# Cross-attention with a routed feed-forward: value products in blocks of two steps, a rewritten unit order, and two steps moved to ScalarE

## The reference

```python
def _L0_xattn_ref(target, source, target_mask, source_mask, Wq, bq, Wk, bk, Wv, bv):
    q = jnp.einsum('oc,bct->bot', Wq, target) + bq[None, :, None]
    k = jnp.einsum('oc,bcs->bos', Wk, source) + bk[None, :, None]
    v = jnp.einsum('oc,bcs->bos', Wv, source) + bv[None, :, None]
    # 16 heads of 16 channels
    dot = jnp.einsum('bhdt,bhds->bhts', q, k) / math.sqrt(HEAD_DIM)
    mask = target_mask[:, :, :, None] * source_mask[:, :, None, :]
    dot = mask * dot - (1.0 - mask) * NEG
    amap = jax.nn.softmax(dot, axis=-1) * mask
    out = jnp.einsum('bhts,bhds->bhdt', amap, v)
    return out.reshape(b, HEADS * HEAD_DIM, t)

def _L0_ffn_ref(hidden_states, gate_w, w1, w2):
    logits = jnp.einsum('th,eh->te', x, gate_w)
    topw, sel = jax.lax.top_k(jax.nn.softmax(logits, axis=-1), 2)
    topw = topw / jnp.sum(topw, axis=-1, keepdims=True)
    g, u = jnp.split(jnp.einsum('th,eoh->eto', x, w1), 2, axis=-1)
    expert_out = jnp.einsum('eti,ehi->eth', jax.nn.silu(g) * u, w2)
    # weighted by topw and summed over the two experts of each row

x = x + _L0_xattn_ref(_layernorm(x), ctx_2048, mask, mask, Wq, bq, Wk, bk, Wv, bv)
x = x + _L0_ffn_ref(_layernorm(x), gate_w, w1, w2)
```

## Time and profile before

| | |
|---|---|
| median of 3 runs | 867.57 us (867.37 to 872.44) |
| the profiled execution | 871.53 us, span 869.7 us |
| TensorE busy | 801.8 us, 92% |
| VectorE busy | 553.6 us, 64% |
| ScalarE busy | 318.6 us, 37% |
| GpSimd busy | 370.3 us, 43% |
| mean granted TensorE clock | 0.972 of full speed |

### The profile page before, as it was taken

The page is one execution under the profiler, slowest core; times in us unless marked ns, Lnnn a source line. Parts: engine busy times, 40 slices in busy tenths (PEclk is TensorE's granted clock), DMA queues, the critical chain, the costliest instruction groups (busy, mean ns, idle before and its releaser), DMA issues. The chain is left out here.

```text
span 869.7 us, 13002 instructions
## 1 busy us (share of the span) xinstructions
PE 801.8 (92%) x3757; PEld 365.1 (42%) x3758; DVE 553.6 (64%) x1071; ACT 318.6 (37%) x619; POOL 370.3 (43%) x392
## 2 busy tenths in 40 slices
PE   5888898989999998999989988899999999999993
PEld 2322332333333433433333332365555665665661
DVE  5778887889888887888877874445433333333331
ACT  0035465556565565665655666522000000000000
POOL 7544364556565655655745423334211221211221
PEclk9579999999999999999999999999999999999997
DMA  6745577666766866856845542354648546354332
GB/s 188 231 129 145 172 203 221 200 209 210 231 206 184 264 196 182 257 163 177 244 127 160 172 113 83 94 144 110 152 89 227 133 110 172 65 156 72 72 51 34
DMA packets 84524, 138.02 MB, mean 159 GB/s; under 512 B 14765, under 2 KB 40685, under 8 KB 84474
## 3 DMA queue, kind: packets, MB, share of 16 engines
q1 hardware_dynamic: 68970, 108.65, 41.8%
q0 software_dynamic: 7744, 17.86, 10.7%
q10 hardware_dynamic: 7760, 10.89, 4.5%
HBM read 77.36 MB, written 59.36 MB: 157 GB/s over the span
## 5 line engine op out<-in xcount | busy, mean ns | idle before, releaser
L843 ACT ACTIVATE pr<-sc 128x512 f32<-128x512 f32 x512 | 267.1, 603 | 219.5 <-PE sc L1507 219.3
L990 DVE TENSOR_REDUCE mx<-tile 128x2 f32<-128x1024 f32 x256 | 309.0, 1216 | 55.9 <-PE tile L1519 50.3
L1507 PE MATMUL sc<-qk 100*128 100x512 bf16 x512 | 154.8, 384 | 9.9 <-DMA qk<-mxt 7.2
L1519 PE MATMUL tile<-qk 97*128 97x512 bf16 x496 | 150.9, 388 | 14.0 <-DVE mx L990 7.9
L765 POOL DMA_INDIRECT out_dram<-xin,ids x36 | 56.4, 1566 | 224.0 <-DVE ids L1312 220.0
L1545 PE MATMUL pvb<-pr,vp 128*32 128x512 f32 x1024 | 138.0, 611 | 0.0
L1660 PE MATMUL pvb<-wring,qkf 128*128 (+1 forms) x216 | 98.7, 593 | 1.6 <-DVE qkf L1322 1.6
L720 POOL TENSOR_SCALAR parts<-qkf 128x512 bf16<-128x512 f32 x31 | 46.9, 1512 | 123.3 <-DVE qkf L1074 119.3
L1519 PEld LDWEIGHTS tile<-qk 97*128 97x128 bf16 x496 | 35.0, 98 | 145.6 <-issue 75.7
L1639 PE MATMUL tile<-wring,xh 128*128 x288 | 91.3, 460 | 0.0
L1639 PE MATMUL sc<-wring,xh 128*128 x288 | 91.2, 459 | 0.0
(11 more groups left out here) (158 smaller groups left out, 789.1 us busy)
## 6 DMA issues: line engine op xcount, KB each, us to landing
qk<-stack_d SPq DMA_DIRECT2D x32, 768.0 KB
stack_d<-parts SPq DMA_DIRECT2D x32, 384.0 KB, 3.1
wring<-w_dram SPq DMA_DIRECT2D x32, 352.0 KB, 7.2
cin<-routed_d ACTq DMA_DIRECT2D x36, 257.0 KB, 3.6
stack_d<-parts SPq DMA_DIRECT2D x32, 256.0 KB, 3.1
pv_d<-ov SPq DMA_DIRECT2D x32, 256.0 KB, 3.4
xin<-x_dram SPq DMA_DIRECT2D x16, 256.0 KB, 5.4
cin<-ctxt_dram SPq DMA_DIRECT2D x8, 512.0 KB, 6.3
```

Source lines behind the costliest of these rows:

```text
L843: nc.scalar.activation(pr[s % 2][:, j, :], sc[(32 * u + 4 * s + j) % NSC][:, :], ACT.Exp, scale=SCALE).then_inc(exped.sem, 1)
L990: dve.tensor_reduce(cols, t[:, :, :], X, ALU.max, negate=True).then_inc(drained.sem, 1)
L1507: nc.tensor.matmul(sc[(32 * u + 4 * s + j) % NSC][:, :], ks[half(u)][0:ALL_ROWS, h, c * P:c * P + P], qs[half(u)][0:ALL_ROWS, h, :], start ...
L1519: last = nc.tensor.matmul(t[:, i, :], qs[half(w)][0:RAW_ROWS, h, c * P:c * P + P], ks[half(w)][0:RAW_ROWS, h, :], start=True, stop=True)
```

## The change

The first two units (`FRONT`) keep their loop, now in `front_events` and `front`. For units 2 to 15, `STEADY` gives the list of tiles, and TensorE's and VectorE's steps are written out. These are the differences:

- products come in blocks of two steps: 6 and 7 of the unit before behind the first scores, 0 and 1 in step 2, 2 and 3 in step 4, 4 and 5 in step 6. `pr` has three buffers for it (`NPR`); the mask rows `mall` and `mrow` now lie in `ov`;
- values move from step 0 to step 1, `xT` into step 4, logits into step 5. The choice stands ahead of the transpose of the maxima, the keys right behind it and ahead of step 7, and two raw pairs at the unit's end. The raw pairs are spread anew;
- ScalarE normalizes the inputs (`normalize`, for which GpSimd's `batch_rstd` makes a third small value, `shift`), behind the exponentials of step 1. VectorE writes the token rows once, and ScalarE copies them for the second expert (`token_twin`), behind the exponentials of step 3. `choose` reads the logits from PSUM without the copy `lg`;
- on VectorE the reciprocals come ahead of the token normalization, and in unit 15 `plan_early` stands ahead of both. On GpSimd `token_rstd` stands ahead of `values_out`. Product 6 of unit 15 too stands behind the first gate.

```diff
+NPR = 3
+STEADY = (0, 1, 2, "v", 3, 4, 5, 6, "q", "xT", 7, 8, 9, 10, "logits", 11, 12, "maxT", "k", 13, "ranks", 14, 15)
...
+def pair_of(n, i):
+    m = LEAD + i
+    return (n + 1, m) if m < NPAIR else (n + 2, m - NPAIR)
...
+def tile_events(n):
+    if 0 <= n < len(FRONT):
+        return front_events(n)
+    ahead = {"v": 1, "q": 3, "k": 3, "xT": -2, "logits": -2, "ranks": -2, "maxT": 1}
+    ev = []
+    for name in STEADY:
+        if name == "xT" and n == TAIL:
             ev.append((n, "early"))
+        if name == "maxT":
+            if has(n + 1):
+                ev.append((n, ("maxT", n + 1, ALL)))
+        elif name in ahead:
+            if has(n + ahead[name]):
+                ev.append((n, name))
+        elif has(pair_of(n, name)[0]):
+            ev.append((n, ("max", *pair_of(n, name))))
+    if n == LAST - 1:
+        ev.append((n, "count"))
...
-        rstd = Count(sem("rstd"), of(5, "eps", "pow"))
+        rstd = Count(sem("rstd"), lambda n: ["eps", "pow"] + ["shift"] * (n > 0) if has(n + 5) else [])
...
+                if u > 0:
+                    pool.wait_ge(rstd.sem, rstd.at(u, "pow"))
+                    pool.tensor_scalar(at[:, 10:11], at[:, 6:7], at[:, 8:9], -1.0, ALU.mult, ALU.mult
+                                       ).then_inc(rstd.sem, 1)
+                    pool.wait_ge(rstd.sem, rstd.at(u, "shift"))
...
                     part(u, 1)
+                if has(u - 2):
+                    token_rstd(u)
                 if has(u + 1):
                     values_out(u)
-                if has(u - 2):
-                    token_rstd(u)
                 if has(u - 3):
...
+            def token_twin(u):
+                act.wait_ge(normed2.sem, normed2.at(u, "n"))
+                nc.scalar.activation(xa[:, half(u), 1, 0:T], xa[:, half(u), 0, 0:T], ACT.Copy
+                                     ).then_inc(twin.sem, 1)
+            def normalize(u):
+                w = u + 5
+                if not has(w):
+                    return
+                at = ln[:, half(w), :]
+                act.wait_ge(rstd.sem, rstd.at(u, "shift"))
+                if (due := ready.at(w - 7 + half(w + 1), "q")) is not None:
+                    act.wait_ge(ready.sem, due)
+                nc.scalar.activation(xh[:, parity(w), half(w), :], xin[:, half(w), :], ACT.Identity,
+                                     bias=at[:, 10:11], scale=at[:, 8:9]).then_inc(normed.sem, 1)
...
-                            if j == 0 and (due := pved.at(u, s, back=2)) is not None:
+                            if j == 0 and (due := pved.at(u, s, back=NPR)) is not None:
                                 act.wait_ge(pved.sem, due)
-                            nc.scalar.activation(pr[s % 2][:, j, :], sc[(32 * u + 4 * s + j) % NSC][:, :],
+                            nc.scalar.activation(pr[(8 * u + s) % NPR][:, j, :], sc[(32 * u + 4 * s + j) % NSC][:, :],
...
+                    if s == 1 and u > 1:
+                        normalize(u - 1)
+                    if s == 3 and has(u - 2):
+                        token_twin(u)
...
-                if step == 0:
-                    dve.tensor_copy(lg[:, :], tile_of(u, "logits")[:, 0, 0:E]).then_inc(drained.sem, 1)
                 if step == 1:
-                    dve.wait_ge(drained.sem, drained.at(u, "logits"))
                     if (due := gate_exp.at(u - 1, "e")) is not None:
                         dve.wait_ge(gate_exp.sem, due)
-                    dve.max(v8[:, :], lg[:, :]).then_inc(choice.sem, 1)
+                    dve.max(v8[:, :], tile_of(u, "logits")[:, 0, 0:E]).then_inc(choice.sem, 1)
                 if step == 2:
                     dve.wait_ge(choice.sem, choice.at(u, "v8"))
-                    dve.max_index(i8[:, :], v8[:, :], lg[:, :]).then_inc(choice.sem, 1)
+                    dve.max_index(i8[:, :], v8[:, :], tile_of(u, "logits")[:, 0, 0:E]).then_inc(drained.sem, 1)
                 if step == 3:
-                    dve.wait_ge(choice.sem, choice.at(u, "i8"))
+                    dve.wait_ge(drained.sem, drained.at(u, "logits"))
                     dve.tensor_copy(i8f[:, :], i8[:, :]).then_inc(choice.sem, 1)
...
-                maximum(u, u + 1, 4)
-                normalize(u - 1)
-                maximum(u, u + 1, 5)
+                maximum(u, *pair_of(u, 0))
+                maximum(u, *pair_of(u, 1))
+                maximum(u, *pair_of(u, 2))
                 values_out(u)
-                maximum(u, u + 1, 6)
+                maximum(u, *pair_of(u, 3))
                 token_stats(u, 0)
-                maximum(u, u + 1, 7)
                 token_stats(u, 1)
-                maximum(u, u + 1, 8)
-                token_normalize(u, 0)
-                maximum(u, u + 1, 9)
-                token_normalize(u, 1)
                 if u == TAIL:
                     plan_early()
-                maximum(u, u + 1, 10)
+                maximum(u, *pair_of(u, 4))
+                maximum(u, *pair_of(u, 5))
                 reciprocals(u, 0)
-                maximum(u, u + 1, 11)
+                maximum(u, *pair_of(u, 6))
                 reciprocals(u, 1)
+                token_normalize(u)
                 projection_out(u, 0)
-                maximum(u, u + 1, 12)
-                maximum(u, u + 1, 13)
+                batch_stats(u, 0)
+                batch_stats(u, 1)
+                maximum(u, *pair_of(u, 7))
+                maximum(u, *pair_of(u, 8))
+                maximum(u, *pair_of(u, 9))
+                maximum(u, *pair_of(u, 10))
                 choose(u, 0)
                 choose(u, 1)
                 choose(u, 2)
                 choose(u, 3)
-                maximum(u, u + 1, 14)
-                batch_stats(u, 0)
-                maximum(u, u + 1, 15)
-                batch_stats(u, 1)
+                maximum(u, *pair_of(u, 11))
+                maximum(u, *pair_of(u, 12))
                 choose(u, 4)
                 choose(u, 5)
+                split_maxima(u, u + 1, ALL)
+                projection_out(u, 1)
+                maximum(u, *pair_of(u, 13))
+                rows_of(u, 0)
+                rows_of(u, 1)
                 if u == TAIL:
                     fetch(0, 0)
-                maximum(u, u + 2, 0)
-                maximum(u, u + 2, 1)
-                split_maxima(u, u + 1, ALL)
-                maximum(u, u + 2, 2)
-                rows_of(u, 0)
-                maximum(u, u + 2, 3)
-                rows_of(u, 1)
-                projection_out(u, 1)
+                maximum(u, *pair_of(u, 14))
+                maximum(u, *pair_of(u, 15))
...
+            def unit(u):
+                scores(u, 0, 0)
+                scores(u, 0, 1)
+                scores(u, 0, 2)
+                raw(u, 0)
+                scores(u, 0, 3)
+                if u > len(FRONT):
+                    product(u - 1, 6)
+                product(u - 1, 7)
+                raw(u, 1)
+                scores(u, 1, 0)
+                raw(u, 2)
+                scores(u, 1, 1)
+                scores(u, 1, 2)
+                scores(u, 1, 3)
+                values(u)
+                raw(u, 3)
+                scores(u, 2, 0)
+                scores(u, 2, 1)
+                scores(u, 2, 2)
+                raw(u, 4)
+                product(u, 0)
+                product(u, 1)
+                if u == TAIL:
+                    count_early()
+                scores(u, 2, 3)
+                raw(u, 5)
+                scores(u, 3, 0)
+                scores(u, 3, 1)
+                raw(u, 6)
+                scores(u, 3, 2)
+                scores(u, 3, 3)
+                project(u, 0)
+                scores(u, 4, 0)
+                scores(u, 4, 1)
+                transpose_tokens(u)
+                scores(u, 4, 2)
+                raw(u, 7)
+                scores(u, 4, 3)
+                raw(u, 8)
+                product(u, 2)
+                product(u, 3)
+                raw(u, 9)
+                scores(u, 5, 0)
+                scores(u, 5, 1)
+                scores(u, 5, 2)
+                raw(u, 10)
+                scores(u, 5, 3)
+                logits(u)
+                scores(u, 6, 0)
+                scores(u, 6, 1)
+                raw(u, 11)
+                scores(u, 6, 2)
+                raw(u, 12)
+                scores(u, 6, 3)
+                product(u, 4)
+                product(u, 5)
+                if has(u + 1):
+                    transpose_maxima(u, u + 1, ALL)
+                project(u, 1)
+                if u == TAIL:
+                    transpose_rows(0, 0)
+                scores(u, 7, 0)
+                raw(u, 13)
+                scores(u, 7, 1)
+                ranks(u)
+                scores(u, 7, 2)
+                scores(u, 7, 3)
+                raw(u, 14)
+                raw(u, 15)
...
+            product(TAIL, 6)
             product(TAIL, 7)
```

110 lines of the change are left out of this document (47 added, 63 removed).

## The result

The changed kernel takes 872.96 us (median of 20 runs, 868.53 to 878.64), the kernel before beside it on the same chip 868.77 us (20 runs, 866.55 to 872.44). The ratio is 1.0044, with a 95% interval of 1.0030 to 1.0057: 3.8 us slower by the ratio, 4.2 by the medians, where 6.6 us of gain were forecast. This is inside the 1% that was taken as "same", but the interval leaves no doubt of the sign, and it is the wrong one.

What follows compares the result with a forecast made beforehand. TensorE plus what it waits for was taken as the bound. Terms of -7.5, -1.1, -0.6 and +2.6 summed to -6.6 us, 864.9 for the profiled run and 861.0 for the median, range 847 to 874.

Steps and rivals of the forecast that it cites:

- Paired product blocks: TensorE, four pairs a unit: two product blocks in a row save 0.19 us a pair, 0.76 us a unit.
- The new unit, walked: Steady units: TensorE's work of 29.0 us plus six waits summing to 1.17 gives 30.2, with 0.2 for the split 30.4 us.
- VectorE's relief, ScalarE's steps: Steps moved off VectorE help TensorE only through the counted waits; ScalarE's two steps cost nothing beyond the counted 0.24 us.
- The denominators: Reciprocals' data in units 3, 5, 7, 9 come 2.1, 1.0, 0.6, 0.3 us late, landing on TensorE in full.
- The slower rival: Denominators as late as in unit 3 in every unit, 2.1 us in 12 units: 882 us; chance 0.08.
- Units 2 to 12 together: Sum of the unit-by-unit gains and losses over these steady units: 7.5 us less.
- Unit 13 and unit 14: Unit 13, without keys over the transpose, takes about 1.1 us less, unit 14 0.6 less.
- Unit 15, a loss: Token normalization behind the early plan and reciprocals delays the token transpose: +2.6 us, bounds 0 to +4.
- From the profiled run to the median: Profiled run's 871.5 was 4.0 us above the median 867.57, put to late landings, so 864.9 became 861.0.
- that the pairs don't save: Rival: paired product blocks save nothing, 56 x 0.19 = 10.6 us come back, 871.6 us; chance 0.08.
- The one on the split: Rival: GpSimd's residual addition holds VectorE's split in every unit, 0.7 us more in 13 units, 870 us; chance 0.12.

Runs made afterwards that it cites:

- e4: Changed kernel with VectorE again writing the token rows for the second expert, instead of ScalarE's copy: 875.89 us, ratio 1.0089 to the kernel before.
- e8: Changed kernel with the input rows' normalization back on VectorE, behind a unit's first maximum: 874.25 us, ratio 1.0079 to the kernel before.
- e13: e7 with 18 unread matmuls ahead of unit 15's token transpose: 869.35 us, ratio 1.0005 to the kernel before.
- e1: Changed kernel with unit 15's token normalization ahead of the early plan on VectorE again: 866.17 us, ratio 0.9982 to the kernel before.
- e7: Kernel before with only unit 15's two token normalizations moved behind the early plan and the reciprocals: 873.61 us, ratio 1.0062.
- e2: Changed kernel with a score, raw pair or maxima's transpose between the two product blocks of each pair: 883.48 us, ratio 1.0176 to the kernel before.
- e18: Kernel before with short fills of unread matmuls at the program's start: 867.77 us, ratio 0.9991.
- e5: e1 with the first gate's rows fetched and transposed earlier in the last unit: 867.68 us, ratio 0.9993 to the kernel before.
- e17: Changed kernel with unit 15's normalization ahead of the plan, first rows early, unit 14's split earlier, fills at start and end: 861.73 us, ratio 0.9922.
- e12: e5 plus fills at start and units 13 to 15, unit 14's split earlier, 48 unread matmuls ahead of the first projection: 864.66 us, ratio 0.9944.

## Why the prediction was wrong, step by step

- **Paired product blocks**: right. 0.23 us saved for each pair instead of 0.19; taking 52 of the 56 apart costs 10.5 to 11.5 us, where 9.9 follow from the forecast's 0.19.
- **The new unit, walked**: right in its sum. 30.4 us forecast, 30.30 to 30.75 in units 6, 8, 10, 11 and 12. The transpose of the maxima has no wait where it waited 1.09. The single waits are not confirmed: unit 10 shows idle time at three places only (0.12 us at a raw pair, 0.11 at the logits, 0.34 at raw pair 14), and matmul records overlap, so shorter waits can't be seen.
- **VectorE's relief, ScalarE's steps**: e4 and e8 are not faster than the changed kernel, which agrees with steps on ScalarE that cost little and a move of the input normalization that brings a little; more is not shown.
- **The denominators**: right in kind, and too small in units 7 and 9. Unit 7 shows them, SyncE, VectorE and TensorE (answers to the earlier trace rows):

```profile
292.59 0.66 SPq L510 DMA_DIRECT2D den<-pv_d  x1
...
294.68 0.35 DVE L1011 RECIPROCAL rec<-den 128x32 f32<-128x32 f32 x1 [1.54 <-DMA den<-pv_d]
...
296.74 0.66 PE L1620 MATMUL tile<-idf,xa 128*128 128x128 f32 x4 [1.12 <-DVE xa L988]
```

The issue is 12.2 us into the unit, where 10.4 plus 0.5 was assumed, VectorE waits 1.54, TensorE 1.12, and the unit takes 31.9. Late by 0.6 was forecast. Against before, units 3, 5, 7 and 9 changed by -0.4, -0.1, +1.0 and +0.2 us, 0.7 in sum instead of nothing. The slower rival that rests on this, 2.1 in every unit, is out: VectorE waits for `den` in units 2, 3, 7 and 9 only.
- **Units 2 to 12 together**: 7.0 gained where 7.5 were forecast, though unit 4 alone lost some 3.3 us to a stretch at 1.2 GHz; units 8 and 11, which before ended on late rows (1.69 us at unit 9's start), gained more than their term.
- **Unit 13 and unit 14**: this step failed. 1.1 and 0.6 us of gain were forecast; they lost 0.9 and 4.1. I took the walked unit's gain over to units that lack the query projection. Without it TensorE comes to the token transpose 0.94 us too early in both units, and in unit 13 to raw pair 14 1.36 us too early. In unit 14 the sum is: 2.9 us at the lower clock (0.09 of 32.56), 0.93 at the token transpose, 0.72 more at the rows (3.41 instead of 2.69), 0.76 less for the pairs. That is 3.8 of the 4.1 us. The largest term, the clock, is the one that is gone from unit 14's start in the seven profiles with the fills.
- **Unit 15, a loss**: the late transpose was foreseen, its price was not. +2.6 was forecast, with a bound of +4; it is +5.9. The transpose was expected at 14.9 us into the unit and stood at 15.8. The clock takes at most 5.1 us of the unit (0.17 of 29.84) instead of 1.7; 1.6 us of the stretch at 543.5 lie in the wait itself, so 4.3 is nearer, 2.6 more than before. The other 3.3 are near the forecast's size, but that the forecast of 2.6 was right for the waits is not shown by this: e13 puts the late order without the lower clock at 0.4 us in the kernel before (at most 2.7), and e1 says that with the clock it costs 5.4 to 6.8 in the changed kernel.
- **Which of the two turned the sign**: either alone would have. With unit 15 at its forecast of +2.6 the profiled span would have been 1.2 us under the kernel before's instead of 2.1 over, with unit 14 at its forecast 2.6 under. e1 shows it for unit 15 by a run.
- **What failed in both**: the sum priced a wait at its own length and left TensorE's clock out, although the windows in the earlier trace rows had a clock of 0.95 in unit 2. Waits of 1 to 3.8 us had stretches of 3.4 to 10.2 us at 1.2 GHz in them or behind them, half of which is lost wherever TensorE is the bound. e13 against e7 shows it for one such wait, the fills support it for unit 14, and for unit 4 it is argued from the rows.
- **From the profiled run to the median**: by the profiled runs the forecast misses by 8.7 us (873.6 where 864.9 was forecast), by the medians by 12.0. The other 3.3 are nearly all of the 4.0 us that I subtracted for late landings: the profiled run of the changed kernel is only 0.6 over its own median, and that of the kernel before 2.8 over its median of 20 runs, not 4.0.

Of the rivals, that the pairs don't save is out (e2). The one on the split is half right. The cast of the split, ns min/median/max:

```profile
L1050 DVE CAST mxt<-mxr x18: 214/555/726, 36.4 to 525.2; 32x128 bf16<-32x128 f32 x14, 16x128 bf16<-16x128 f32 x4
```

It takes 0.47 to 0.68 us in every unit from 2 to 14, up to the end of GpSimd's addition, so it is held in every unit, as that rival said. But the steady units don't pay its 0.7 us: units 8, 10, 11 and 12 last 30.4 to 30.8 and not 31.1, and TensorE isn't seen idle ahead of their next unit's first score for more than 0.17 us.

## What to carry to other kernels

Price a wait of TensorE by what the granted clock does behind it, not by its length alone: look through the windows for stretches at 1.2 GHz, see which wait each begins in or behind, and ask whether a new order puts another wait near it. Do this over several profiles, since the places differ from run to run. The last units, where work thins out, are the place for this, and an order that holds in the steady units has to be walked again there. A clock that rises brings nothing where another engine sets the pace (e18), so first find out who waits for whom.

## What was not expected of the hardware

- Short waits of TensorE can have a long stretch behind them: unit 4's 0.34 and 1.04 us, then 6.8 us at 1.2 GHz. But the same wait does not always: e5 waits 1.29 us at unit 4's first score and has 6.8 us at 1.2 GHz there, e8 and e17 wait 1.39 and 1.36 and have none. The changed kernel's runs have clocks between 0.961 and 0.971.
- In the profile of e12 the first projection of an idle engine took 1.98 us with matmuls ahead of it, where the changed kernel's takes 3.69 without. The view prints a granted clock of 1.00 in both windows, but the trace of the changed kernel has no entry of the clock ahead of 11.06 us, just where these four matmuls end, and that of e12 has none ahead of 7.57. So the 1.00 ahead of the first entry isn't a reading.
- VectorE's selection `sel` takes 0.35 to 0.79 us under GpSimd's tensor_tensor in units 2 to 12 and 1.21 and 1.15 in units 13 and 14, where 0.18 is its time without one (unit 15). It is the holding of the earlier trace rows on another instruction.
